# End of an expert stage on one Trainium2 core: the mixed bias as products of its own, and the scale products two tiles to a bank

## The reference, cut to what matters

```
out = zeros_like(x)
for g in range(G):                        # G = 4
    ...                                   # iw: two of 8 experts per group
    y = _layernorm(z + moe, gln_g[g], gln_b[g])
    out = out + gw[:, g:g+1] * y          # gw has two non-zero groups per token
return out.reshape(b, t, d) + inp
```

## Time and profile before

| | us |
|---|---|
| median of 3 runs | 2302.05 |
| lowest and highest of the 3 | 2300.82, 2307.59 |
| the profiled execution, whole | 2290.77 |
| its span, first to last instruction | 2289.0 |
| its mean granted TensorE clock, as a share of full speed | 0.909 |

### The profile page before, as it was taken

The page is one execution under the profiler, slowest core; times in us unless marked ns, Lnnn a source line. Parts: engine busy times, 40 slices in busy tenths (PEclk is TensorE's granted clock), DMA queues, the critical chain, the costliest instruction groups (busy, mean ns, idle before and its releaser), DMA issues. The chain is left out here.

```text
span 2289.0 us, 44262 instructions
## 1 busy us (share of the span) xinstructions
PE 1994.3 (87%) x14601; PEld 1440.8 (63%) x14601; DVE 1331.5 (58%) x4494; ACT 1171.7 (51%) x2507; POOL 779.3 (34%) x973
## 2 busy tenths in 40 slices
PE   5699999999999999999998878888876459999986
PEld 4366666666666666666666546656554349999973
DVE  2365565556556655565566645777766625555547
ACT  2376666566666665665666324555644224444434
POOL 0012221222122212221223221234787745555556
PEclk8799999999999999999999885798877579999995
DMA  3642441244134513440350124342321277777654
GB/s 101 123 72 28 70 71 38 34 70 70 33 40 70 94 30 43 70 69 27 47 88 11 34 70 83 86 92 49 80 57 37 76 247 234 231 228 228 200 157 129
DMA packets 113846, 207.06 MB, mean 90 GB/s; under 512 B 23060, under 2 KB 47510, under 8 KB 112968
## 3 DMA queue, kind: packets, MB, share of 16 engines
q1 hardware_dynamic: 100632, 182.97, 36.0%
q0 software_dynamic: 10176, 17.09, 2.3%
q10 hardware_dynamic: 2816, 4.16, 0.6%
HBM read 147.53 MB, written 64.66 MB: 93 GB/s over the span
## 5 line engine op out<-in xcount | busy, mean ns | idle before, releaser
L733 ACT ACTIVATE tower_prob<-tower_prob,tower_negmax 128x386 f32<-128x386 f32 (+1 forms) x768 | 390.5, 556 | 312.0 <-DVE tower_negmax L943 311.4
L943 DVE CUSTOM_DVE_ANT_0 tower_prob<-seam_sbank,tower_band 128x386 f32<-128x386 f32 (+1 forms) x768 | 346.1, 488 | 138.7 <-PE seam_sbank L496 133.3
L534 PEld LDWEIGHTS seam_tbank<-sh_ident,tower_prob 128*128 128x128 f32 x1920 | 226.3, 142 | 131.0 <-issue 81.0
L534 PE MATMUL seam_tbank<-sh_ident,tower_prob 128*128 128x128 f32 x1920 | 283.0, 278 | 23.5 <-DVE seam_probT L968 21.3
L789 ACT ACTIVATE seam_probT<-seam_tbank 128x384 f32<-128x384 f32 (+1 forms) x576 | 227.5, 430 | 123.6 <-PE seam_tbank L534 121.3
L2186 POOL DMA_INDIRECT scratch_yt<-experts_y,experts_rows x190 | 186.7, 983 | 183.6 <-DVE experts_y L2329 151.1
L473 PE MATMUL seam_dbank<-tower_oxT,tower_w 96*128 96x512 f32 x384 | 190.9, 621 | 14.7 <-ACT tower_oxT L778 14.7
L496 PE MATMUL seam_sbank<-seam_k_st,seam_q_st 49*128 49x386 f32 (+1 forms) x768 | 160.1, 411 | 30.0 <-POOL seam_k_st L684 16.3
L2244 PE MATMUL experts_ybank<-experts_w,experts_hid 128*128 128x128 f32 x1520 | 185.1, 275 | 0.0
L2232 PE MATMUL experts_hbank<-experts_zT,experts_w 128*128 128x256 f32 x760 | 181.5, 382 | 1.1 <-ACT experts_zT L2268 1.1
L2277 ACT ACTIVATE experts_hid<-experts_hbank,experts_w 128x256 f32<-128x256 f32 x190 | 79.8, 471 | 193.9 <-PE experts_hbank L2232 193.9
(11 more groups left out here) (329 smaller groups left out, 3441.0 us busy)
## 6 DMA issues: line engine op xcount, KB each, us to landing
experts_w<-ew SPq DMA_DIRECT2D x95, 578.0 KB, 4.0
scratch_qk<-seam_qk SPq DMA_DIRECT2D x64, 384.0 KB, 4.7
seam_q_st<-scratch_qk SPq DMA_DIRECT2D x96, 192.0 KB, 8.3
seam_k_st<-scratch_qk SPq DMA_DIRECT2D x96, 192.0 KB, 11.6
experts_rows<-scratch_zs SPq DMA_DIRECT2D x95, 132.0 KB
scratch_kq<-seam_qk SPq DMA_DIRECT2D x8, 1024.0 KB, 4.3
experts_res<-scratch_yt SPq DMA_DIRECT2D x8, 1024.0 KB, 7.9
seam_q_st<-scratch_kq SPq DMA_DIRECT2D x48, 128.0 KB, 4.3
```

The lines of the kernel that those rows point to most:

```text
L534: mm = pe.transpose(bank[:, jb * P:jb * P + P], prob[:, hg % PR, at + jb * P:at + jb * P + P], ident[:, :])
L733: act.activation(prob[:, hg % PR, 0:width(i)], prob[:, hg % PR, 0:width(i)], ACT.Exp, bias=negmax[:, hg % PR:hg % PR + 1], scale=-1.0).the ...
L943: scores.copied(dve.tensor_tensor_reduce(prob[:, hg % PR, 0:width(i)], bank[:, 0:width(i)], band[:, BAND_AT[i]:BAND_AT[i] + width(i)], sca ...
```

## The change

The three products of a tile (scale, scale, bias: 384 columns) are taken apart. The bias rows become products of their own: one bank for each sequence, four calls of 128 columns each, all eight sequences one after the other ahead of any scale product. DVE adds each bank to `out` with one operation of 512 columns, ahead of `gathered(0)`, and waits for its eight additions. The scale rows of two tiles share a bank (two calls of 256 columns), and DVE multiplies `m` with one operation of 512 columns for each bank, two for a sequence in place of four. The order of the ring is now mix 0 to 7, bias 0 to 7, and gl (b, k).

```diff
-                   + [("mix", b) for b in range(B)] + [("gl", t) for t in range(NTT)], "up_")
+                   + [("mix", b) for b in range(B)] + [("bias", b) for b in range(B)]
+                   + [("gl", b, k) for b in range(B) for k in HALVES], "up_")
...
             for b in range(B):
                 up.wait_copied(pe, ("mix", b))
-            for t in range(NTT):
-                bank = up.claim(pe, ("gl", t))
-                up.filled(pe.matmul(bank[:, 0:3 * E], mixed[:, t * P:t * P + P], glmix[:, :], start=True, stop=True),
-                          ("gl", t))
+                bank = up.claim(pe, ("bias", b))
+                for t in range(TC):
+                    at = (TC * b + t) * P
+                    mm = pe.matmul(bank[:, t * E:t * E + E], mixed[:, at:at + P], glmix[:, 2 * E:3 * E],
+                                   start=True, stop=True)
+                up.filled(mm, ("bias", b))
+            for b in range(B):
+                for k in HALVES:
+                    bank = up.claim(pe, ("gl", b, k))
+                    for j in range(2):
+                        at = (TC * b + 2 * k + j) * P
+                        mm = pe.matmul(bank[:, 2 * E * j:2 * E * j + 2 * E], mixed[:, at:at + P], glmix[:, 0:2 * E],
+                                       start=True, stop=True)
+                    up.filled(mm, ("gl", b, k))
...
             dve.wait_ge(base_in, 16)
+            for b in range(B):
+                bank = up.take(dve, ("bias", b))
+                rows_b = out[:, TC * b:TC * b + TC, :].rearrange("p t d -> p (t d)")
+                up.copied(dve.tensor_tensor(rows_b, rows_b, bank[:, :], ALU.add), ("bias", b))
+            for b in range(B):
+                up.wait_copied(dve, ("bias", b))
...
-                for t in range(TC):
-                    bank = up.take(dve, ("gl", TC * b + t))
-                    dve.tensor_tensor(out[:, TC * b + t, :], out[:, TC * b + t, :], bank[:, 2 * E:3 * E], ALU.add)
-                    up.copied(dve.tensor_tensor(mb[:, t, :, :], mb[:, t, :, :],
-                                                bank[:, 0:2 * E].rearrange("p (j d) -> p j d", j=2), ALU.mult),
-                              ("gl", TC * b + t))
-                for t in range(TC):
-                    up.wait_copied(dve, ("gl", TC * b + t))
+                for k in HALVES:
+                    bank = up.take(dve, ("gl", b, k))
+                    pairs = mb[:, 2 * k:2 * k + 2, :, :].rearrange("p t j d -> p (t j d)")
+                    up.copied(dve.tensor_tensor(pairs, pairs, bank[:, :], ALU.mult), ("gl", b, k))
+                for k in HALVES:
+                    up.wait_copied(dve, ("gl", b, k))
```

## The result

| | before | changed |
|---|---|---|
| median of 19 runs each, us | 2298.93 | 2291.21 |
| lowest and highest, us | 2293.24, 2308.86 | 2286.84, 2302.26 |
| span of the profiled execution, us | 2289.0 | 2288.4 |
| DVE's last operation of the blocks ends at, us | 2216.52 | 2220.84 |
| from there to the end of the last addition ("the end"), us | 69.18 | 64.87 |

The ratio is 0.9973, with a 95% interval of 0.996 to 0.9986: the changed kernel is faster, by 3.2 to 9.2 us. The two profiled spans differ by 0.6 us only, and that hides the gain: the changed kernel's execution reached the end of the blocks 4.3 us later, in code that the change doesn't touch.

A forecast was written before the change was run, and what follows sets the result against it. Bound by a chain of waits over POOL, ACT and DVE, 12.97 us a turn of two sequences. Taking out 4.7 us and adding 1.8 gives 2.9 less: 2302.05 to 2299.1 us, range 2294.5 to 2304.0.

The forecast's parts named there:

- The base: Whole kernel: median of three runs, 2302.05 us, from which the saving was taken; median trusted to perhaps 1.5 us either way.
- The gain: End of the stage: 4.7 us taken out, 1.8 us added by the later chain start, net 2.9 us less.
- mixed_in 0.90 shorter: mixed_in on DVE: two 512-column multiplications replace four pairs, 1.44 for 2.34 us; whole mixed_in 2.85 for 3.75.
- POOL's waits move: POOL's roots beside DVE's additions: some 0.37 us gained for each turn, a turn 11.70 in place of 12.97 us.
- The power doesn't hold the addition: POOL's power beside DVE's first last addition of the odd sequence: the meeting was costed at nothing.
- rival (c): POOL's power holds DVE's addition 0.5 us each turn: net about -1.7 us, 2300.4; chance 0.08.
- The bias ahead of gathered(0): PE's bias banks at half clock, 1.89 us each: gathered(0) 2.05 us late, the chain starts 1.8 us later.
- (a) full clock: PE's clock stays at 1.00 through the bias products, so the bias is hidden: -4.7 us, 2297.3; chance 0.24.
- (b): PE at half clock from the first bias bank: roots of 0 4.9 us late, +0.2 us, 2302.3; chance 0.11.
- (d): PE's weight loads don't overlap the bias products: 0.56 us an instruction, chain 26 us late, 2323; chance 0.03.
- (e): mixed_in's 512-column multiplications save nothing, PSUM reads being slower over a whole bank: +1.8 us or less, 2303.9; chance 0.04.
- Faster, the same or slower: Whole kernel: chance 0.10 of faster by over 0.3%, 0.85 within 0.3%, 0.05 slower by over 0.3%.

The follow-up runs named there:

- The second profile of before: The kernel before, run again with no edit: end 69.27 us against 69.18 the first time, span 2307.4 us, ratio 1.0001.
- The changed kernel again: The changed kernel, run again with no edit: end 65.05 us, ratio 0.9983 (0.9963 to 1.0004) to the kernel before.
- the doubled products: The changed kernel with every bias product made twice into the same place: gathered(0) starts at 27.81 us, end 78.52 us.

## Why the prediction was wrong, point by point

The mechanism held; what failed are sizes. Two terms were mis-sized: the base, allowed an error of 1.5 us and off by 3.1, and the delay that the bias puts ahead of gathered(0), forecast as 1.8 us and measured as 0.8. A third stood at nothing: 0.6 us behind the last addition. The time missed by 7.9 us (2299.1 against 2291.21). The chance of 0.10 was for more than 0.3%: the medians show 0.34%, the ratio 0.27%, with an interval down to 0.14%, so the runs don't decide whether that happened. Three things make up the 7.9:

- **The base, 3.1 us.** The prediction stood on the median of three runs, 2302.05; over 19 runs it is 2298.93. The prediction named the scatter (6.8 us) but allowed the median only 1.5. The second profile of before shows where such scatter lies: 16.0 of its 18.4 us ahead of the expert stage, with a lower granted clock there. Even 17 to 35 runs gave medians 7 us apart, so 1.5 for three runs was too narrow.
- **The gain, 2.0 us too small** (2.9 against 4.9). By terms: what is taken out was forecast as 4.7 and measured as 5.1 (the delay of 0.8 added to the 4.3 of the end); the added delay as 1.8 and measured as 0.8; and 0.6 lies behind the last addition, where the prediction had nothing.
- **The rest, 2.8 us** (7.7 between the medians, 4.9 in the profiles). The changed kernel again gave 0.9983 and 1.8 us between medians, and at the same clock the two kernels differ by what the end gives. I take it as scatter of the medians. With the base put right the forecast would have been 2296.0, inside the range; with the gain too, 2294.0, just below 2294.5. The rest of the miss is this scatter.

The steps:

- *mixed_in 0.90 shorter.* 0.95: 2.80 in place of the forecast 2.85. Right.
- *POOL's waits move.* Right, nearly to the tenth: odd mixed_in at +2.64 (2248.72 less 2246.08; forecast +2.65) and held back by its norm, the even norm at +5.58 (forecast +5.63), a turn of 11.60 (11.70), the last leg 16.43 (16.49). L2213 is held in both halves, as forecast.
- *The power doesn't hold the addition.* Right: L2371 starts at 2250.11, while L2209 (2248.99 to 2250.66) runs, and takes 0.69 all the same; rival (c) is out. (The row that the prediction read for it, L1805, is a multiplication and not an addition. It too has two inputs in SBUF, so the reading stood.) The Trainium skill's rule of one owner for a whole instruction ("SBUF — State Buffer", "SBUF: two separate sides") isn't borne out for the power, while it agrees with the pair sums, which held one of DVE's additions (2.72 for 0.69) and its negation (2.34).
- *The bias ahead of gathered(0).* The mechanism was right: PE at half clock delivers late, the idle time before gathered(0) is ended by the bias. The size was off: **delay 0.8 in place of 1.8.** The prediction took 1.89 us a bank from products of another shape with 96 rows; these took 1.70. That is four times 0.19, and the clock fell 0.5 us later in the stage, worth half of that: 1.0 of the 1.08 us by which gathered(0) came earlier than forecast (14.14 against 15.22). When it falls differs from run to run: 5.1 to 6.2 us into the end in the thirteen profiles. gathered(0) goes with it by up to 0.6: it starts at 13.73, 14.14 and 14.33 with the fall at 6.2, 5.8 and 5.6.
- *(a) full clock*: refuted, by PE busy without a gap through the fall, and by the doubled products. *(b)* didn't happen: the clock was at 1.00 for the first 3.5 us of the bias products. *(d)*: an instruction took 0.17 us on average (10.87 over 64) and 0.21 at clock 0.50 (1.70 over 8), under the 0.34 from which it decides; the weight loads overlap (PEld is busy for 2.00 of 2.00 us beside PE). *(e)*: refuted, 1.28 for two multiplications.
- *Faster, the same or slower.* 0.85 for within 0.3% rested on an upper bound of 6.1 for the gain, and the profiles keep under it. What the chances lacked is the width of the medians themselves.

What stays open in part is the 0.6 us behind the last addition: 3.30 and 3.25 in the two profiles of before, 2.69 to 2.75 in all eleven others, with and without the bias products and whatever the buffers. DMA issues and the instruction queue (q14) in 2280 to 2289 us, before (first two lines) and after:

```profile
q14 instruction: 1, 0.01, 0.4%
out<-experts_out SPq DMA_DIRECT2D x2, 256.0 KB, 2.6
```

```profile
out<-experts_out SPq DMA_DIRECT2D x2, 256.0 KB, 2.3
```

The 2.6 is the median of two stores: the last one alone lands 2.8 us from its issue in both profiles of before and 2.3 in all the others. In both profiles of before one packet of the instruction queue falls beside that store, and in none of the others does one fall in the last 3.3 us. That goes with 0.5 of the 0.6 us; no run moves this packet alone, so the cause isn't shown.

## What to carry to other kernels

Where a chain closes over several engines, lay out one turn of it from the rows, with every engine's start counted from the same event: it gave the changed turn to 0.1 us of 11.6, holds between engines included. Moving work off such a chain pays only as far as the place it moves to is really idle; look at which engine delivers it and at what clock, and take the price from a row of the same shape and rows. And compare medians only with the scatter known: when the profiled stretch repeats to 0.1 us and whole runs scatter over 15, the stretch is the measure, and the range of a forecast must carry the error of the base. Where the scatter goes with the granted clock, compare runs at the same clock.

## What the runs showed of the hardware that was not expected

- An operation of 8 columns on DVE with a single SBUF input took 2.34 us when it met POOL's sum of 1024 columns. The same negation on ACT took 0.19 to 0.21 us each time, also beside POOL's sum (0.21 at 2251.60).
- A short POOL operation that starts in the last 0.1 us of one DVE addition and just ahead of the next isn't held and doesn't hold: L2211 at 2250.73 took 0.20, between L2371 (2250.11, 0.69) and L2372 (2250.83, 0.69).
- With products of 8 rows the clock fell under a PE that was busy without a gap: 1.00 in 2224 to 2226 us, 0.50 in 2228 to 2230. With twice as many products it stayed at 0.50 through 24.5 us of them, less the first 3.5. The Trainium skill ("TensorE: Matmul & The Clock Gate", "Part 1: The HAM clock gate") ties the clock to how busy the engine has been; busy time as the profile counts it is not that.
- A fourth buffer made the stage longer (66.01 in place of 64.09), because the wait it removed had kept two engines out of each other's way: POOL's sum met one addition of DVE, 2.72 us in place of 0.69.
